# Product keys: the output product of the last group in two column ranges, and batch 14 weighed on VectorE

## The chip, the cores and the metric

One Trainium2 chip, one of its cores. The metric is the device time of one execution in microseconds (us), the median of several. The core has five engines with a queue each: TensorE (PE in the profile; PEld is its weight load), VectorE (DVE), ScalarE (ACT), GpSimd (POOL) and SyncE (SP).

## The reference, cut to what matters

The kernel is four layers of cross attention and feed-forward on x (16 batches of 128 tokens of 128 numbers). The change touches one stage, the feed-forward part of layer 2, which looks up experts by product keys:

```python
def _L2_ffn_ref(x, w_q, keys, expert_down, expert_up, norm_w):
    xn = _rmsnorm(x, norm_w)                                   # 2048 tokens x 128
    q = (xn @ w_q.T).reshape(b, t, H, 2, DK)                   # H=8 heads, two halves
    sim1 = jnp.einsum('bthd,hkd->bthk', q[..., 0, :], keys[:, :, 0, :])   # 32 keys
    sim2 = jnp.einsum('bthd,hkd->bthk', q[..., 1, :], keys[:, :, 1, :])   # 32 keys
    s1, i1 = jax.lax.top_k(sim1, K)
    s2, i2 = jax.lax.top_k(sim2, K)
    # the K*K sums s1+s2, of which the K best pairs (k1, k2) pick experts 32*k1 + k2
    wd = expert_down[fi]
    wu = expert_up[fi]
    hidden = jax.nn.gelu(jnp.einsum('btd,bthkd->bthk', xn, wd), approximate=False)
    hidden = hidden * jax.nn.relu(fs)
    return jnp.einsum('bthk,bthkd->btd', hidden, wu)
```

## The kernel before

The program is a chain of stages, each a block of its own: the engines' queues are joined at the end of one, and the next begins when all are through. The stage here is `product_keys` (l2f in the names). It computes the hidden value of all 1024 experts for each token, weighs each with what the chosen pairs give it, and multiplies the result by the 1024 x 128 output matrix.

Names: B = 16 batches, in four groups g of GB = 4 (batch b is number q = b % 4 of group b // 4). K = 32 keys a side, and P = S = D = 128. Per batch b:

- PE `score(b)` (line 2569) makes the similarities. DVE and POOL pick the eight best of each side and the threshold of the pairs (`tops`, `parts`, `threshold`, `compare`, and the tensor_tensor operations of POOL), and DVE turns the factors of both sides (`turn`, lines 2804 and 2810).
- ACT `spread(b)` (line 2663) copies the right factor into four diagonal blocks. It waits for the turn and for the `give` before (`given_made`), since `blocks` is one buffer.
- PE `give(b)` (line 2593) multiplies both factors: 32 matmuls in fp32, into `given_ps`, one buffer, so it also waits until batch b - 1 has been read out of it.
- The weighing multiplies `hid[g % 2][:, :, q, :]` by `given_ps`. Batches with q = 0 and 3 are weighed by DVE straight from PSUM (line 2781). Those with q = 1 and 2 (`ON_POOL`) go by way of ACT, which copies `given_ps` to SBUF (`store_given`, line 2669), and POOL multiplies (line 2714).
- `hide(g, c)` (line 2580) and ACT's Gelu make the hidden values of a whole group ahead of it.
- When the four batches of a group are weighed, PE `project_out(g)` (line 2605) multiplies by the output matrix: 32 keys k, and for each the four row groups j of 32 partitions, 128 matmuls with weights of 32 x 128 (`w["up"][rows, k, :]`) and 128 moving columns (four batches of 32 columns), summed over k in four banks of PSUM. ACT `store_out` (line 2677) copies the four banks, PE `finish(g)` (line 2616) transposes, DVE `add(g)` (line 2817, with the row statistics at lines 120 and 123) adds to x.

The order on each engine is written by hand, by rounds i = 0 to 19 (`ROUNDS`): in round i DVE does `parts`, `threshold` and `compare` of batch i, weighs batch i - 2, and turns batch i. PE gives batch i - 1. `project_out(3)` stands in round 17, `finish(3)` in round 18. `work_ps` has four banks, which `hid`, `out` and `finish` uses take in turn (`uses`, `place`, `wait_free`); the last use of a bank before `project_out(3)` is `finish(2)`, which `add(2)` on DVE frees. An fp32 matmul stands in the trace as two records of PE and two of PEld: 128 matmuls are x256.

Of the kernel before, what the change touches and what calls it, by code (L numbers as in the profile page):

```python
# [13 lines left out]
B, S, D = 16, 128, 128  # L14
# [14 lines left out]
NCH = B * S // CH  # L29
# [2423 lines left out]
def product_keys(nc, m, w, tag, meanwhile):  # L2453

    H, K, GB, TERMS = 8, 32, 4, 4
    KK, WORK = K // GB, 4
    ON_POOL = (1, 2)
    FAR = 1.0e30
    x, xnT, identity = m["x"], m["xnT"], m["identity"]
    with cleared_semaphores(nc) as new_semaphore, ExitStack() as ctx:  # L2460
# [63 lines left out]
        def bank(use):  # L2524
            return work_ps[place[use] % WORK]

        def wait_free(eng, use):
            n = place[use]
            if n >= WORK:
                eng.wait_ge(work_freed[n % WORK], n // WORK)  # L2530
# [13 lines left out]
        def exists(b):  # L2544
            return 0 <= b < B

        def on_pool(b):
            return b % GB in ON_POOL

        def count(b, pool):  # L2550
            return sum(on_pool(c) == pool for c in range(b))
# [9 lines left out]
        @block.tensor  # L2561
        def _(pe):
            mm = nc.tensor.matmul

            def score(b):
                norm.wait_stored(pe, b // GB)
                if b >= 2:
                    pe.wait_ge(parts_made, b - 1)
                mm(sim_ps[b % 2].rearrange("p h j k -> p (h j k)"), xnT[:, b, :], m["fold"][:, :],  # L2569
                   start=True, stop=True).then_inc(sim_made, 1)  # L2570

            def hide(g, c):
                use = ("hid", g, c)
                wait_free(pe, use)
                if g == 0 and c == 2:
                    norm.wait_stored(pe, NCH - 1)
                tokens = xnT[:, GB * g:GB * g + GB, :].rearrange("p q (u j s) -> p j (q u) s", u=4, j=4)
                for k in range(4):
                    for j in range(4):
                        ins = mm(bank(use)[K * j:K * j + K, k, :], w["down"][:, 4 * c + k, :], tokens[:, j],  # L2580
                                 start=True, stop=True)
                fill(ins, use)

            def give(b):
                pe.wait_ge(left_turned, b + 1)
                pe.wait_ge(blocks_made, 4 * b + 4)
                if b and on_pool(b - 1):
                    pe.wait_ge(given_stored, count(b, True))
                elif b:
                    pe.wait_ge(weighted, count(b, False))  # L2590
                for s in range(8):
                    for j in range(4):
                        ins = mm(given_ps[K * j:K * j + K, s, :, :], left_t[b % 2][:, 8 * j + s, :],  # L2593
                                 blocks[:, 8 * j + s, :, :], start=True, stop=True)
                ins.then_inc(given_made, 1)

            def project_out(g):
                for j in range(4):
                    wait_free(pe, ("out", g, j))
                pe.wait_ge(weighted, count(GB * g + GB, False))  # L2600
                pe.wait_ge(weighted_pool, count(GB * g + GB, True))
                for k in range(K):
                    for j in range(4):
                        rows = slice(K * j, K * j + K)
                        ins = mm(bank(("out", g, j))[:, 0, :], w["up"][rows, k, :], hid[g % 2][rows, k, :, :],
                                 start=(k == 0), stop=(k == K - 1))
                        if k == K - 1:
                            fill(ins, ("out", g, j))

            def finish(g):  # L2610
                use = ("finish", g, 0)
                for j in range(4):
                    wait_freed(pe, ("out", g, j))
                wait_free(pe, use)
                for q in range(GB):
                    ins = nc.tensor.transpose(bank(use)[:, q, :], out_t[:, q, :], identity[:, :])
                fill(ins, use)

            norm.pe(pe, 0)
            norm.pe(pe, 1)  # L2620
            score(0)
            norm.pe(pe, 2)
            norm.pe(pe, 3)
            score(1)
            for c in range(KK):
                hide(0, c)
            for i in ROUNDS:
                for g, c in chunks(i):
                    hide(g, c)
                if exists(i + 2):  # L2630
                    score(i + 2)
                if exists(i - 1):
                    give(i - 1)
                if out_group(i) is not None:
                    project_out(out_group(i))
                if i and out_group(i - 1) is not None:
                    finish(out_group(i - 1))
# [60 lines left out]
        @block.gpsimd  # L2698
        def _(pool):
            TT = nc.gpsimd.tensor_tensor  # L2700

            def wide(a):
                return a.unsqueeze(2).broadcast_to([P, H, 2, K])

            def each(a):
                return a.unsqueeze(3).broadcast_to([P, H, 2, K])

            def weigh(b):
                g, q = b // GB, b % GB
                if q == ON_POOL[0]:  # L2710
                    gelu_done(pool, b)
                pool.wait_ge(given_stored, count(b + 1, True))
                hidden = hid[g % 2][:, :, q, :].rearrange("p k (u s) -> p k u s", u=4)
                TT(hidden, hidden, given_sb.rearrange("p s u k -> p k u s"), ALU.mult).then_inc(weighted_pool, 1)

            norm.pool(pool)
            nc.gpsimd.memset(pairs[:, :, 28:36], 0.0).then_inc(zeroed, 1)
            nc.gpsimd.memset(blocks[:, :, :, :], 0.0).then_inc(zeroed, 1)
            for b in range(B):
                pool.wait_ge(top_made, b + 1)  # L2720
                if b:
                    pool.wait_ge(best_made, b)
                TT(pairs[:, :, 0:16].rearrange("p h (a c) -> p h a c", a=2),
                   top[:, :, 0, 0:2].unsqueeze(3).broadcast_to([P, H, 2, 8]),
                   top[:, :, 1, :].unsqueeze(2).broadcast_to([P, H, 2, 8]), ALU.add).then_inc(pairs_made, 1)
                TT(pairs[:, :, 16:28].rearrange("p h (a c) -> p h a c", a=6),
                   top[:, :, 0, 2:8].unsqueeze(3).broadcast_to([P, H, 6, 2]),
                   top[:, :, 1, 0:2].unsqueeze(2).broadcast_to([P, H, 6, 2]), ALU.add).then_inc(pairs_made, 1)
                if b:
                    pool.wait_ge(right_turned, b)  # L2730
                    pool.wait_ge(left_turned, b)
                TT(factors[:, 1, :, 0:2 * K].rearrange("p h (f k) -> p h f k", k=K),
                   wide(second_sim[b % 2][:, :, :]), each(top[:, :, 0, 0:2]), ALU.add).then_inc(sums_made, 1)
                pool.wait_ge(parts_made, b + 1)
                TT(factors[:, 0, :, 2 * K:4 * K].rearrange("p h (f k) -> p h f k", k=K),
                   wide(others[:, :, :]), each(top[:, :, 1, 0:2]), ALU.add).then_inc(sums_made, 1)
                for n, side in enumerate((1, 0)):
                    hot = factors[:, side, :, 2 * K * side:2 * K * side + K]
                    second = factors[:, side, :, 2 * K * side + K:2 * K * side + 2 * K]
                    TT(second, second, hot, ALU.subtract).then_inc(split_made, 1)  # L2740
                    value = factors[:, side, :, 2 * K * (1 - side):2 * K * (1 - side) + 2 * K]
                    pool.wait_ge(kept_made, 2 * b + n + 1)
                    TT(value, value, kept[:, side, :, :], ALU.mult).then_inc(cut_made, 1)  # L2743
                if exists(b - 2) and on_pool(b - 2):
                    weigh(b - 2)
            weigh(B - 2)
            row_stats.scale_known(pool)

        @block.vector
        def _(dve):  # L2750
# [72 lines left out]
            for i in ROUNDS:  # L2823
                if exists(i):
                    parts(i)
                    threshold(i)
                    compare(i)
                if exists(i - 2) and not on_pool(i - 2):
                    weigh(i - 2)
                if exists(i + 1):  # L2830
                    tops(i + 1)
                if exists(i):
                    turn(i)
                if i >= 2 and out_group(i - 2) is not None:
                    add(out_group(i - 2))


# [297 lines left out]
```

## Time and profile before

| | us |
|---|---|
| median of 3 runs | 1182.0 |
| lowest, highest | 1180.79, 1188.72 |
| the profiled execution | 1187.32 |
| its span (first to last instruction) | 1185.6 |
| the stage `product_keys` in it | about 840 to 1047 |

The rows further down are times of the profiled execution, counted from the start of its span. "x64" counts records, "mean ns" or "min/median/max" is the duration of one record. A released wait is printed behind a row in brackets with the instruction that ended it.

### The profile page before, as it was taken

What the parts mean: (1) busy time and instruction counts of PE and PEld (TensorE: products, weight loads), DVE (VectorE), ACT (ScalarE), POOL (GpSimd) and SP (SyncE); (2) the same over time, 40 slices, a digit from 0 to 9 for tenths busy, and PEclk for the clock granted to TensorE, in tenths of its full rate; (3) what the DMA queues carried; (4) which work ended last, traced back from release to release, by engine and by line L of the source; (5) the groups of instructions that cost most, each with busy time, mean ns of one, the idle gap of its engine ahead of it and who ended that gap; (6) DMA issues with size and microseconds to landing.
All of it is one profiled execution on the core that took longest, in us unless ns stands there. A gap on an engine that the chain in (4) does not pass through costs nothing. (4 is left out here: it accounts for less than half of the span.)

```text
span 1185.6 us, 26637 instructions
## 1 busy us (share of the span) xinstructions
PE 948.0 (80%) x10747; PEld 617.9 (52%) x10777; DVE 740.0 (62%) x2026; ACT 583.8 (49%) x956; POOL 414.4 (35%) x426
## 2 busy tenths in 40 slices
PE   3999799998999986998798781777556677479997
PEld 1577433443333433677676381445345555446776
DVE  3587747557455564654375233478899999636764
ACT  3365365535555344554563460377555555325442
POOL 4230300000000011676201656246578878623340
PEclk9799699998999998999898796899778987789997
DMA  6000000000000007000000132100000000000001
GB/s 268 1 3 2 19 1 0 1 1 0 1 1 1 0 1 288 10 2 3 2 3 2 36 110 56 72 1 1 1 2 2 2 2 3 2 1 2 2 2 37
DMA packets 15434, 27.95 MB, mean 24 GB/s; under 512 B 1104, under 2 KB 13264, under 8 KB 14544
## 3 DMA queue, kind: packets, MB, share of 16 engines
q1 hardware_dynamic: 14288, 24.14, 5.7%
q0 software_dynamic: 1024, 2.10, 0.6%
q8 instruction: 87, 1.43, 0.5%
q14 instruction: 35, 0.29, 0.1%
HBM read 20.33 MB, written 5.90 MB: 22 GB/s over the span
## 5 line engine op out<-in xcount | busy, mean ns | idle before, releaser
L1324 PE MATMUL l0f_ctl<-l1f_in,l0f_in 128*128 128x512 f32 x320 | 145.7, 599 | 0.5
L128 POOL TENSOR_SCALAR row_var_eps<-row_mean_var 128x12 f32<-128x12 f32 (+2 forms) x16 | 3.7, 230 | 358.5 <-DVE row_mean_var L123 357.7
L548 DVE TENSOR_REDUCE l_neg_max<-l_ring 128x4 f32<-128x512 f32 x128 | 82.1, 684 | 66.1 <-PE l_ring L410 65.6
L507 ACT ACTIVATE l_probs<-l_scores 128x1024 f32<-128x1024 f32 x64 | 65.6, 1025 | 82.2 <-PE l_scores L418 82.2
L2663 ACT COPY l2f_blocks_sb<-l2f_right_t_sb 32x1024 f32<-32x1024 f32 x64 | 66.8, 1044 | 68.2 <-DVE l2f_right_t_sb L2804 33.8
L1324 PEld LDWEIGHTS l0f_ctl<-l1f_in,l0f_in 128*128 128x128 f32 x320 | 61.7, 193 | 71.5 <-issue 70.2
L2593 PE MATMUL l2f_given_ps<-l2f_blocks_sb,l2f_left_t_sb 128*32 128x128 f32 x1024 | 47.8, 364 | 33.1 <-ACT l1f_in L2669 22.6
L698 POOL TENSOR_TENSOR l_squares<-l_exps 128x1024 f32<-128x1024 f32 x32 | 60.6, 1895 | 29.8 <-ACT l_exps L953 29.8
L2593 PEld LDWEIGHTS l2f_given_ps<-l2f_blocks_sb,l2f_left_t_sb 128*32 128x32 f32 x1024 | 42.8, 150 | 47.1 <-issue 46.9
L1045 DVE TENSOR_REDUCE l_neg_max<-l_scores 128x8 f32<-128x1024 f32 x32 | 39.2, 1225 | 43.4 <-PE l_scores L750 43.4
L368 POOL TENSOR_SCALAR_AFFINE_SELECT l_probs<-l_probs 128x1024 f32<-128x1024 f32 x32 | 35.0, 1094 | 64.1 <-ACT l_probs L507 64.1
L1597 DVE TENSOR_SCALAR l0f_halt<-l0f_halt 128x512 f32<-128x512 f32 x8 | 3.4, 427 | 78.8 <-ACT l0f_halt L1483 78.8
L1590 DVE SCALAR_TENSOR_TENSOR l1f_in<-l0f_index,l0f_in,l0f_hidden 128x512 f32<-128x512 bf16 x64 | 43.5, 747 | 12.3 <-ACT l0f_index L1464 11.1
L2743 POOL TENSOR_TENSOR l2f_factors_sb<-l2f_factors_sb,l1f_in 128x512 f32<-128x512 f32 x32 | 48.0, 1500 | 0.0
L953 ACT ACTIVATE l_exps<-l_scores 128x1024 f32<-128x1024 f32 x32 | 32.8, 1025 | 30.0 <-PE l_scores L756 29.8
L410 PE MATMUL l_ring<-l_k_heads,l_q_all 32*128 32x256 f32 x256 | 41.0, 441 | 7.9 <-issue 3.2
L1324 PE MATMUL l0f_work<-xnT,l0f_in 128*128 128x512 f32 (+2 forms) x88 | 45.0, 684 | 1.3 <-ACT xnT L204 0.7
L750 PE MATMUL l_scores<-l_k_heads,l_q_all 32*128 32x256 f32 x256 | 36.8, 402 | 10.0 <-DVE l_neg_max L1045 8.3
L2569 PE MATMUL l2f_sim_ps<-l1f_in,xnT 128*128 128x512 f32 x32 | 21.6, 764 | 28.8 <-DVE l1f_in L2772 28.8
L1446 ACT ACTIVATE l0f_hidden<-l0f_work,l0f_in 128x512 f32<-128x512 f32 (+1 forms) x40 | 27.3, 686 | 29.0 <-PE l0f_work L1324 29.0
L992 ACT ACTIVATE l_exps<-l_scores 128x1024 f32<-128x1024 f32 x32 | 31.0, 1021 | 20.7 <-PE l_scores L837 20.7
L756 PE MATMUL l_scores<-l_q_all,l_k_heads 32*128 32x128 f32 x512 | 37.7, 286 | 1.8 <-ACT l_exps L953 1.8
(458 smaller groups left out, 2610.2 us busy)
## 6 DMA issues: line engine op xcount, KB each, us to landing
l1f_in<-in_l1f SPq DMA_DIRECT2D x1, 4580.0 KB, 13.4
l0f_in<-in_l0f SPq DMA_DIRECT2D x1, 2302.5 KB, 8.9
l0f_in<-in_l2f SPq DMA_DIRECT2D x1, 2080.5 KB, 18.7
l1f_in<-in_l2u SPq DMA_DIRECT2D x1, 2048.0 KB, 8.6
sorted_rows<-first_in SPq DMA_DIRECT2D x1, 1856.0 KB, 11.2
l1f_sorted<-sorted_rows SPq DMA_DIRECT2D x7, 256.0 KB, 4.6
expert_rows<-l1f_sorted SPq DMA_DIRECT2D x7, 256.0 KB, 2.2
x_in<-in_x SPq DMA_DIRECT2D x1, 1024.0 KB, 5.0
```

The lines of the kernel that those rows point to most:

```text
L410: ins1 = mm(score_bank(b, half, g)[:, :, t, :], q_all[r, b, t, :], k_heads[r, b, t, :, :], start=not causal, stop=True, skip_group_check=True)
L507: nc.scalar.activation(probs[c % 2][:, 2 * pair:2 * pair + 2], scores2[:, :, :, :, :], ACT.Exp, scale=SCORE_SCALE).then_inc(exp_done, 1)
L548: ring.free(V.tensor_reduce(out, score_bank(b, half, g), AX.X, ALU.max, negate=True), ("score", b, half, g))
L698: nc.gpsimd.tensor_tensor(squares[c % 2][:, pair], e, e, ALU.mult).then_inc(squared, 1)
L750: ins1 = mm(scores1[:, g, :, t, :], q_all[r, b, t, :], k_heads[r, b, t, :, :], start=True, stop=True, skip_group_check=True)
L756: ins2 = mm(scores2[:, g, j, t, :], k_heads[r, c, t, j, :], q_all[r, c, t, :], start=True, stop=True, skip_group_check=True)
L1045: V.tensor_reduce(out, scores1[:, :, :, :, :].rearrange("p g j t s -> p (g j) t s"), AX.X, ALU.max, negate=True).then_inc(max_taken, 1)
L1324: return nc.tensor.matmul(out, lhs, rhs, start=start, stop=stop)
L1590: ins = STT(chosen[c % 2][:, k, p, :], index[k][:, c % 2, :], w["row_expert"][:, p:p + 1], hidden[c % 2][:, p, :], ALU.is_equal, ALU.mult)
L2593: ins = mm(given_ps[K * j:K * j + K, s, :, :], left_t[b % 2][:, 8 * j + s, :], blocks[:, 8 * j + s, :, :], start=True, stop=True)
L2663: A.copy(blocks[rows, :, u, :], right_t[rows, :, :]).then_inc(blocks_made, 1)
L2743: TT(value, value, kept[:, side, :, :], ALU.mult).then_inc(cut_made, 1)
```

## The change

Three things are changed. Batch 14 (q = 2 of the last group) is weighed by DVE, and the copy on ACT and the multiplication on POOL for it are gone. DVE's `add(2)` moves from round 15 to round 16, behind that weighing. `project_out(3)` becomes three calls: the columns of batches 12 to 14 for keys 0 to 11 (`EARLY_KEYS`) in round 16 ahead of `give(15)`; the same columns for keys 12 to 31 in round 17, behind `give(15)`; and the 32 columns of batch 15 for all 32 keys behind that. The four banks are waited for by the first call, and each call waits for the weighing of its own batches.

```diff
-    ON_POOL = (1, 2)
+    ON_POOL, EARLY_KEYS = (1, 2), 12
...
         def on_pool(b):
-            return b % GB in ON_POOL
+            return b % GB in ON_POOL and b != B - 2
...
-            def project_out(g):
-                for j in range(4):
-                    wait_free(pe, ("out", g, j))
-                pe.wait_ge(weighted, count(GB * g + GB, False))
-                pe.wait_ge(weighted_pool, count(GB * g + GB, True))
-                for k in range(K):
+            def project_out(g, batches=range(GB), keys=range(K)):
+                if batches[0] == 0 and keys[0] == 0:
+                    for j in range(4):
+                        wait_free(pe, ("out", g, j))
+                pe.wait_ge(weighted, count(GB * g + batches[-1] + 1, False))
+                pe.wait_ge(weighted_pool, count(GB * g + batches[-1] + 1, True))
+                some = slice(batches[0], batches[-1] + 1)
+                cols = slice(K * batches[0], K * batches[-1] + K)
+                for k in keys:
                     for j in range(4):
                         rows = slice(K * j, K * j + K)
-                        ins = mm(bank(("out", g, j))[:, 0, :], w["up"][rows, k, :], hid[g % 2][rows, k, :, :],
+                        ins = mm(bank(("out", g, j))[:, 0, cols], w["up"][rows, k, :], hid[g % 2][rows, k, some, :],
                                  start=(k == 0), stop=(k == K - 1))
-                        if k == K - 1:
+                        if k == K - 1 and batches[-1] == GB - 1:
                             fill(ins, ("out", g, j))
...
+                if i == B:
+                    project_out(NCH - 1, range(GB - 1), range(EARLY_KEYS))
                 if exists(i - 1):
                     give(i - 1)
-                if out_group(i) is not None:
+                if out_group(i) == NCH - 1:
+                    project_out(NCH - 1, range(GB - 1), range(EARLY_KEYS, K))
+                    project_out(NCH - 1, range(GB - 1, GB))
+                elif out_group(i) is not None:
                     project_out(out_group(i))
...
-            weigh(B - 2)
             row_stats.scale_known(pool)
...
-                if i >= 2 and out_group(i - 2) is not None:
+                if i == B:
+                    add(out_group(i - 3))
+                elif i >= 2 and out_group(i - 2) is not None and i != B - 1:
                     add(out_group(i - 2))
```

PE's queue at the end of the stage, before, from the `give` of batch 13 on (rows are line, operation, output<-inputs, shape, count; `l2f_given_ps` is written by `give`, `l2f_work_ps` by `project_out` and `finish`):

```order
L2593 MATMUL l2f_given_ps<-l2f_blocks_sb,l2f_left_t_sb 32x128 x32
L2616 MATMUL l2f_work_ps<-first_in,l1f_in 128x128 x4
L2593 MATMUL l2f_given_ps<-l2f_blocks_sb,l2f_left_t_sb 32x128 x64
L2605 MATMUL l2f_work_ps<-l2f_hid_sb,l1f_in 128x128 x128
L2616 MATMUL l2f_work_ps<-first_in,l1f_in 128x128 x4
L2460 UNCONDITIONAL_BRANCH
```

The same place now; the line numbers have moved by three:

```order
L2593 MATMUL l2f_given_ps<-l2f_blocks_sb,l2f_left_t_sb 32x128 x32
L2619 MATMUL l2f_work_ps<-first_in,l1f_in 128x128 x4
L2593 MATMUL l2f_given_ps<-l2f_blocks_sb,l2f_left_t_sb 32x128 x32
L2608 MATMUL l2f_work_ps<-l2f_hid_sb,l1f_in 128x96 x48
L2593 MATMUL l2f_given_ps<-l2f_blocks_sb,l2f_left_t_sb 32x128 x32
L2608 MATMUL l2f_work_ps<-l2f_hid_sb,l1f_in 128x96 x80
L2608 MATMUL l2f_work_ps<-l2f_hid_sb,l1f_in 128x32 x128
L2619 MATMUL l2f_work_ps<-first_in,l1f_in 128x128 x4
L2460 UNCONDITIONAL_BRANCH
```

Forty-eight matmuls of 96 columns stand ahead of the last `give` (batch 15), and behind it the 128 matmuls of the output product have become 80 of 96 columns and 128 of 32 columns.

DVE's queue at the end of the stage, before, from the turn of batch 15 on:

```order
L2804 STREAM_TRANSPOSE l2f_right_t_sb<-l2f_factors_sb 128x32x32
L2810 STREAM_TRANSPOSE l2f_left_t_sb<-l2f_factors_sb 128x32x32
L2817 TENSOR_TENSOR x_in<-x_in,l2f_work_ps 128x512
L120 BN_STATS row_stats<-x_in 128x6 x4
L123 BN_AGGR row_mean_var<-row_stats 128x2 x4
L2781 TENSOR_TENSOR l2f_hid_sb<-l2f_hid_sb,l2f_given_ps 128x32x32
```

and now, where lines 2788, 2811, 2817 and 2824 are the former 2781, 2804, 2810 and 2817:

```order
L2811 STREAM_TRANSPOSE l2f_right_t_sb<-l2f_factors_sb 128x32x32
L2817 STREAM_TRANSPOSE l2f_left_t_sb<-l2f_factors_sb 128x32x32
L2788 TENSOR_TENSOR l2f_hid_sb<-l2f_hid_sb,l2f_given_ps 128x32x32
L2824 TENSOR_TENSOR x_in<-x_in,l2f_work_ps 128x512
L120 BN_STATS row_stats<-x_in 128x6 x4
L123 BN_AGGR row_mean_var<-row_stats 128x2 x4
L2788 TENSOR_TENSOR l2f_hid_sb<-l2f_hid_sb,l2f_given_ps 128x32x32
```

The weighing of batch 14 has come in between the turn of batch 15 and `add(2)`; the weighing of batch 15 is last in both.

## Rows read from the trace of the kernel before

**Rows 1.** The page: busy us of each engine, share of the span, instructions.

```profile
PE 948.0 (80%) x10747; PEld 617.9 (52%) x10777; DVE 740.0 (62%) x2026; ACT 583.8 (49%) x956; POOL 414.4 (35%) x426
```

**Rows 2.** Stretches of the stage: us, busy per engine (records), granted clock, DMA.

```profile
840.00:1047.10 207.10, 135.06 (x3136) 110.38 (x3136) 185.03 (x553) 105.28 (x144) 151.19 (x144) 0.83 0.01 2
1019.70:1029.70 10.00, 3.52 (x64) 3.21 (x64) 7.12 (x13) 5.18 (x5) 7.16 (x6) 0.67 0.01 2
```

**Rows 3.** The timeline, PE, end of the stage: start us, us, what [idle before].

```profile
1019.82 3.52 PE L2593 MATMUL l2f_given_ps<-l2f_blocks_sb,l2f_left_t_sb 128*32 128x128 f32 x64 [6.36 <-ACT l1f_in L2669]
1029.76 3.64 PE L2593 MATMUL l2f_given_ps<-l2f_blocks_sb,l2f_left_t_sb 128*32 128x128 f32 x64 [6.41 <-ACT l1f_in L2669]
1034.92 7.43 PE L2605 MATMUL l2f_work_ps<-l2f_hid_sb,l1f_in 32*128 32x128 f32 x256 [1.53 <-DVE l2f_hid_sb L2781]
1043.53 0.60 PE L2616 MATMUL l2f_work_ps<-first_in,l1f_in 128*128 128x128 f32 x4 [1.18 <-ACT l1f_in L2677]
```

**Rows 4.** The timeline, DVE, the same stretch and the next stage's start.

```profile
1024.18 2.08 DVE L2810 STREAM_TRANSPOSE l2f_left_t_sb<-l2f_factors_sb 128x1024 f32<-128x1024 f32 x1
1026.11 0.70 DVE L2817 TENSOR_TENSOR x_in<-x_in,l2f_work_ps 128x512 f32<-128x512 f32 x1
...
1033.45 1.22 DVE L2781 TENSOR_TENSOR l2f_hid_sb<-l2f_hid_sb,l2f_given_ps 128x1024 f32<-128x1024 f32 x1 [5.33 <-PE l2f_given_ps L2593]
1044.16 0.69 DVE L2817 TENSOR_TENSOR x_in<-x_in,l2f_work_ps 128x512 f32<-128x512 f32 x1 [9.49 <-PE l2f_work_ps L2616]
...
1047.14 3.73 DVE L179 TENSOR_SCALAR l_probs<-x_in,row_mean_var,row_rstd 128x128 f32<-128x128 f32 x13 [0.98 <-PEq L43]
```

**Rows 5.** The timeline, ACT, the same stretch.

```profile
1024.33 4.25 ACT L2663 COPY l2f_blocks_sb<-l2f_right_t_sb 32x1024 f32<-32x1024 f32 x4 [4.65 <-DVE l2f_right_t_sb L2804]
1028.60 1.01 ACT L2669 COPY l1f_in<-l2f_given_ps 128x1024 f32<-128x1024 f32 x1
1042.39 0.78 ACT L2677 COPY l1f_in<-l2f_work_ps 128x128 f32<-128x128 f32 x4 [12.78 <-PE l2f_work_ps L2605]
```

**Rows 6.** The timeline, POOL, the same stretch: batch 13, batch 14, statistics.

```profile
1023.96 2.89 POOL L2714 TENSOR_TENSOR l2f_hid_sb<-l2f_hid_sb,l1f_in 128x1024 f32<-128x1024 f32 x1
1029.69 2.87 POOL L2714 TENSOR_TENSOR l2f_hid_sb<-l2f_hid_sb,l1f_in 128x1024 f32<-128x1024 f32 x1 [2.84 <-ACT l1f_in L2669]
...
1032.93 2.29 POOL L131 TENSOR_TENSOR row_rstd<-row_var_eps,first_in 128x12 f32<-128x12 f32 x1
```

**Rows 7.** Short stretches (columns as in rows 2): the granted clock.

```profile
1023.00:1023.40 0.40, 0.34 (x11) 0.01 (x1) 0.40 (x1) 0.00 (x0) 0.40 (x1) 0.89 0.00 0
1026.50:1027.00 0.50, 0.00 (x0) 0.00 (x0) 0.47 (x2) 0.50 (x1) 0.35 (x1) 0.50 0.00 0
1033.00:1033.40 0.40, 0.40 (x8) 0.00 (x0) 0.00 (x0) 0.00 (x0) 0.40 (x1) 0.59 0.00 0
1034.90:1042.30 7.40, 7.38 (x256) 7.26 (x256) 0.00 (x0) 0.00 (x0) 0.32 (x1) 1.00 0.02 4
```

**Rows 8.** The timeline, PE: a `give` in a busy stretch.

```profile
968.80 1.96 PE L2593 MATMUL l2f_given_ps<-l2f_blocks_sb,l2f_left_t_sb 128*32 128x128 f32 x64
```

**Rows 9.** The timeline, PE: weights of 128 x 128, moving 128 and 32.

```profile
1169.96 1.50 PE L2046 MATMUL l3f_turn_ps<-l3f_in,xnT 128*128 128x128 f32 x12
825.11 3.76 PE L2330 MATMUL l_counts<-l0f_in 128*128 128x32 f32 x32
```

**Rows 10.** One line's forms (durations min/median/max): two weight loads and a short matmul.

```profile
L2605 PEld LDWEIGHTS l2f_work_ps<-l2f_hid_sb,l1f_in x1024: 181/187/333, 912.5 to 1042.0; 32*128 32x128 f32 x171
L2330 PEld LDWEIGHTS l_counts<-l0f_in x32: 191/192/272, 825.0 to 828.5; 128*128 128x128 f32 x32
L1324 PE MATMUL l0f_ctl<-l0f_in,l0f_route x32: 356/356/378, 140.3 to 142.7; 32*128 32x8 f32 x32
```

**Rows 11.** Short stretches of line 1324 alone: us, PE, PEld, granted clock, DMA.

```profile
141.40:141.60 0.20, 0.20 (x11) 0.20 (x10) 0.50 0.00 0
141.60:141.80 0.20, 0.20 (x10) 0.20 (x12) 0.50 0.00 0
```

## The prediction

> **What bounds the kernel now.** The page comes first: PE is the busiest engine, at 80% of the span [rows 1]. That is an average over many stages, so the stretches of the stage come next: from 840 to 1047 us DVE is busy for 185 of 207 us and PE for 135 [rows 2]. In the rounds DVE leads, but the change touches only their end, and there the timeline of each engine has to be read side by side. The reader should see one chain with nothing beside it. PE gives batch 15 from 1029.76 to 1033.40 [rows 3]; DVE weighs it from 1033.45 to 1034.67 after 5.33 us of idleness [rows 4]; PE starts the output product at 1034.92, 0.25 us later, and ends at 1042.35 [rows 3]; ACT copies at 1042.39 [rows 5]; PE transposes at 1043.53 [rows 3]; DVE adds at 1044.16, and the next stage's first work on DVE is at 1047.14 [rows 4]. The queues are joined there, so whatever moves the end of the output product moves everything after it by as much. In the chain stand two stretches in which PE sits idle, 6.41 us ahead of the last `give` and 1.53 us ahead of the product, and one slow piece: the `give` takes 3.64 us, against 1.96 us for the same 64 records in a busy stretch [rows 3, 8]. The granted clock is 0.50 (1.2 GHz) after the idle time and 1.00 (2.4 GHz) in the whole of the output product [rows 7].
>
> **The copy and POOL's product for batch 14.** `give` of batch 15 waits for `given_ps` to be free. The copy on ACT that frees it stands behind `spread`, from 1028.60 to 1029.61, and PE starts 0.15 us after it [rows 3, 5]. With DVE reading `given_ps` instead, the `give` would be ready when `spread` ends, 1028.58 [rows 5], so at about 1028.7: 1.05 us earlier. POOL loses 2.87 us that ended at 1032.56, while the batch after it was not weighed until 1034.67 [rows 4, 6]: worth nothing. DVE gains one weighing of 1.22 us, which fits into its 5.33 us of idleness [rows 4]: it costs nothing itself.
>
> **The weighing of batch 14 and `add(2)` on DVE.** The factors are turned by 1026.1, when `add(2)` starts now [rows 4], and the `give` of batch 14 is through at 1023.34 [rows 3]. So DVE weighs from 1026.1 to 1027.3 and adds to 1028.0 (0.70 us). Behind it the statistics end near 1029.3, and POOL needs 2.5 us from them (its last row takes 2.29 us [rows 6]), done by 1032: hidden by 14 us of other work.
>
> **The early piece.** It waits for the weighing of batch 14 and for its four banks, the last of which `add(2)` frees at 1028.0. With the 0.25 us seen between DVE and PE [rows 3, 4] it starts at 1028.2, half a us before `give` of batch 15 would be ready. It stands ahead of the `give` in PE's queue, so all of it delays the `give`. It has 48 matmuls, 96 records. What is one worth? The 256 records of the output product take 7.43 us; their weight loads stand 28 ns apart ((7.26 - 0.187) / 255) [rows 3, 7, 10]. At half clock that is 53 ns: the short matmuls of line 1324 last 356 ns each, and 10 or 11 of them are to be seen in a stretch of 0.20 us at clock 0.50, so a new one starts every (200 + 356) / 10.5 = 53 ns [rows 10, 11].
>
> The clock fell to 0.50 by 1026.50 [rows 7], so the early piece starts at half speed. After the start at 1019.82 the stretch up to 1023.40 shows a mean of 0.89, so 78% of it is at full clock: the first 3.3 us of that `give` ran at half clock. Of the next one, from 1029.76, the mean of 0.59 makes it the first 3.6 us [rows 3, 7]. I take 3.4 us of half clock here too, up to 1031.6. Until then 3.4 / 0.053 = 64 records go through, the other 32 take 0.9 us, and the `give` can follow at 1032.5. It then runs at full clock: 1.96 us instead of 3.64 [rows 3, 8]. It ends at about 1034.4, **1.0 us later** than before. The bounds: at full clock from the first record the early piece takes 2.7 us and the `give` ends at 1032.8 (0.6 us earlier); at half clock throughout it takes 5.1 us and the `give` ends at 1035.2 (1.8 us later).
>
> **The rest of the output product.** Before, 8.95 us lay between the end of `give` and the end of the product: 1.52 us for the weighing and 7.43 us of PE. Now the 80 matmuls of 96 columns follow the `give` at once, and the weighing of batch 15 (1.5 us with its hand-overs) hides behind them. But the last piece is again 128 matmuls, 256 records, each with a weight load of its own. Whether it takes a quarter of the time because it moves a quarter of the columns, or the same time, is the question that decides this change. The trace of before has no matmul with 32 rows of weights and 32 columns. The nearest rows all say that the weight load sets the pace. A full 128 x 128 load with 128 moving columns takes 1.50 us for 12 records, and with 32 moving columns 3.76 us for 32 [rows 9]: less the last record's length (some 0.28 us) 111 and 112 ns each. The columns make no difference. A load of 32 rows lasts 187 ns against 191 for 128 rows [rows 10], so fewer rows don't shorten it either; the four row groups load side by side, and 112 / 4 = 28 ns is what the product shows. And line 1324 with only 8 moving columns keeps 53 ns at half clock, twice 27 [rows 10, 11]. So I take 28 ns for both widths: 160 records 4.5 us, 256 records 7.2 us, and 0.1 us for the last record's end, 11.8 us in place of 8.95: **2.85 us more**. The splitting adds 256 records to 256, takes 96 of them out ahead of the `give`, and saves only 1.5 us of waiting. The bounds of this term: by columns alone (21 and 7 ns) it is 5.3 us, 3.65 less than before; with each load and its columns one after the other it is 16.1 us, 7.15 more.
>
> The Trainium skill (TensorE: Matmul & The Clock Gate, section "Wait — 56ns, not 53.3ns?") says that matmuls never start closer than about 25 ns however few columns they have. By it alone the last piece would be 6.4 us, and the sum 0.8 us smaller. No row here has so short a matmul at full clock in all four row groups, so this trace neither confirms nor refutes the figure.
>
> **The sum.** The product ends 1.0 + 2.85 = 3.85 us later, near 1046.2 instead of 1042.35. The copies, transposes, addition and join behind it are the same. Against the profiled execution (1187.32, span 1185.6) this gives 1191.2; that execution was 5.3 us above the median of 1182.0, and the same difference on the median gives **1185.8 us**. With the bounds of the clock alone the difference is 2.2 to 4.7 us.
>
> **The rivals.** *Columns set the price* (the change ends faster): if a record of the output product costs its columns, 96 cost 21 ns and 32 cost 7 ns (40 ns for 96 at half clock). The early piece then ends near 1031.8 and the `give` near 1033.8, 0.4 us later than before, and the rest takes 5.3 us: 0.4 - 3.65 = 3.25 us faster, 1178.8 us. For it speaks that with 128 columns the load and the columns may well take equally long, so that the 28 ns of the product alone can't tell which of them it is; against it, rows 9 and 11. The Trainium skill gives this rival in the same page, section Back-to-back issue gap: the isolated gap at full clock is N / 2.4 + 2.5 ns, which falls with the columns. The rows 9 speak against using it where every matmul loads weights.
>
> *Loads come into the open* (clearly slower): with few columns to stream, the next load of the same row group may no longer lie beside them. Each record would cost its load and its columns in turn: 47 ns for 96 and 34 ns for 32, 16.1 us for the rest, and some 2 us more in the early piece: about 10 us slower in all, 1192 us. It decides if the product's records after `give` stand over 30 ns apart. The equal spacing of 128 and 32 columns at a full load [rows 9] speaks against it.
>
> *The net is nothing*: if the clock is granted soon after the early piece begins and the records go somewhat closer than 28 ns, the loss is 0 to 2 us and can't be seen: 1183 us. That the change does nothing at all is excluded, since PE's queue is different.
>
> **How the numbers follow.** My forecast has a chance of 0.72, columns 0.12, the net of nothing 0.09, open loads 0.04; 0.03 is left for a change of the clock in later stages. The three runs of before lie 7.9 us apart, so the median of after can miss by 2 or 3 us without a cause. The range of 1179 to 1191 takes in the forecast with the bounds of the clock, the net of nothing and most of the columns' case. A difference within 1% (12 us) can't be told from none by so few runs, and none of the cases but an upset beyond them reaches it: faster 0.02, same 0.95, slower 0.03.
>
> **What would show it.** In the profile after: the early piece at 1028 us or so, 96 records in 4 to 5 us at a clock that begins at 0.50; the `give` behind it near 2 us instead of 3.64; DVE's last weighing inside the 96-column stretch, with no idle PE between; the two stretches behind the `give` at 4.5 and 7.2 us; the end of the product some 12 us after the `give`. If the 256 records of 32 columns take 2 us, or over 8, the step on weight loads is wrong. If the early piece takes under 3 us, the one on the clock is.

## The result, and the profile after

The changed kernel took 1194.4 us in the median (four runs, 1191.2 to 1202.7) against 1182.7 for the kernel before: a ratio of 1.0086 with a 95% interval of 1.0049 to 1.0123 (the two medians by themselves stand 0.99% apart). Measured once more among the experiments it was 1.0046 (1.0015 to 1.0077). Neither interval holds 1, so the changed kernel is slower, by some 0.5 to 0.9%, 5.4 to 10 us. The forecast was 1185.8, a loss of 3.85 us, with a range from 1179 to 1191: the sign was right, the loss about one and a half to two and a half times as large as said. One execution whose trace is read below, that of the wide last piece, was 1.6% slower than the fastest of its kernel, so only what lies within the stage is read from it.

The end of the stage in the trace of the changed kernel, PE first (start us, us, what, idle before it and its releaser). These rows answer to [rows 3]. The row of 416 records merges the 96-column and the 32-column matmuls behind the `give`.

```profile
1015.93 3.53 PE L2593 MATMUL l2f_given_ps<-l2f_blocks_sb,l2f_left_t_sb 128*32 128x128 f32 x64 [6.35 <-ACT l1f_in L2677]
1024.37 5.33 PE L2608 MATMUL l2f_work_ps<-l2f_hid_sb,l1f_in 32*128 32x96 f32 x96 [4.91 <-DVE x_in L2824]
1029.63 1.96 PE L2593 MATMUL l2f_given_ps<-l2f_blocks_sb,l2f_left_t_sb 128*32 128x128 f32 x64
1031.52 15.01 PE L2608 MATMUL l2f_work_ps<-l2f_hid_sb,l1f_in 32*128 32x96 f32 x416
1047.61 1.08 PE L2619 MATMUL l2f_work_ps<-first_in,l1f_in 128*128 128x128 f32 x4 [1.09 <-ACT l1f_in L2685]
```

DVE in the same stretch, which answers to [rows 4]:

```profile
1022.24 1.17 DVE L2788 TENSOR_TENSOR l2f_hid_sb<-l2f_hid_sb,l2f_given_ps 128x1024 f32<-128x1024 f32 x1
1023.34 0.67 DVE L2824 TENSOR_TENSOR x_in<-x_in,l2f_work_ps 128x512 f32<-128x512 f32 x1
...
1031.66 1.22 DVE L2788 TENSOR_TENSOR l2f_hid_sb<-l2f_hid_sb,l2f_given_ps 128x1024 f32<-128x1024 f32 x1 [6.33 <-PE l2f_given_ps L2593]
1048.73 0.69 DVE L2824 TENSOR_TENSOR x_in<-x_in,l2f_work_ps 128x512 f32<-128x512 f32 x1 [15.86 <-PE l2f_work_ps L2619]
...
1051.72 6.78 DVE L179 TENSOR_SCALAR l_probs<-x_in,row_mean_var,row_rstd 128x128 f32<-128x128 f32 x13 [0.98 <-PEq L43]
```

The two profiled executions reach this place at different times, so the ruler for everything below is a distance within a trace: from the start of the `give` of batch 14 to the end of the output product. Before, it is 1019.82 to 1042.35, 22.5 us [rows 3]; after, it is 1015.93 to 1046.53, 30.6 us: 8.1 us more. Another 0.4 us is lost behind it, from there to the next stage's first work on DVE (4.8 us before, 5.2 us after), since the four transposes take 1.08 us instead of 0.60. That makes 8.5 us. The span grew by only 3.9 us, because the stage had begun 4.1 us earlier in that execution (DVE's first work in it at 836.31, before at 840.42) and the later stages took 0.7 us less. The code of those stages is the same in both kernels, so this is the spread between executions. The stage by itself took 206.7 us before (DVE's first work at 840.42, that of the next stage at 1047.14) and 215.4 us in both profiles of the changed kernel: 8.7 us more.

Where the 8.1 us went is seen in short stretches of the same trace (us; PE, PEld, DVE, ACT, POOL busy with records; granted clock; DMA): the early piece, the `give`, the 96 columns, and then the 32 columns in three stretches.

```profile
1024.30:1029.40 5.10, 5.03 (x95) 5.06 (x96) 0.99 (x8) 0.37 (x1) 2.48 (x2) 0.50 0.01 3
1029.60:1031.50 1.90, 1.90 (x68) 1.69 (x64) 0.00 (x0) 0.00 (x0) 0.00 (x0) 1.00 0.00 0
1031.50:1036.00 4.50, 4.50 (x164) 4.48 (x164) 1.22 (x1) 0.00 (x0) 0.00 (x0) 1.00 0.01 4
1036.00:1039.50 3.50, 3.50 (x139) 3.50 (x132) 0.00 (x0) 0.00 (x0) 0.00 (x0) 1.00 0.02 5
1039.50:1040.50 1.00, 1.00 (x32) 1.00 (x31) 0.00 (x0) 0.00 (x0) 0.00 (x0) 0.60 0.06 16
1040.50:1046.50 6.00, 6.00 (x116) 5.89 (x112) 0.00 (x0) 0.00 (x0) 0.00 (x0) 0.50 0.00 0
```

The granted clock, third from the right, is the thing to read. PE is busy for the whole of the last three stretches, with nothing to wait for, and the clock still falls from 1.00 to 0.50 near 1039.7, 3.7 us after the 32-column matmuls began. Until then 132 loads go through in 3.5 us, 27 ns each; afterwards 112 in 6 us, 53 to 54 ns each. The instructions of the product's line show it in the length of one load, first between 1037 and 1039, then between 1041 and 1046 (durations in ns min/median/max, first and last start):

```profile
L2608 PEld LDWEIGHTS l2f_work_ps<-l2f_hid_sb,l1f_in x78: 187/187/187, 1036.9 to 1039.0; 32*128 32x128 f32 x78
```

```profile
L2608 PEld LDWEIGHTS l2f_work_ps<-l2f_hid_sb,l1f_in x100: 328/328/328, 1040.7 to 1045.8; 32*128 32x128 f32 x100
```

### The profile page after: what moved, and what is told of

It reads as the page before. It is cut to its first block and busy times, and to the rows that moved or that the text cites. A ratio compares the mean times of both kernels' runs of the same rounds, so it can differ in the third digit from the quotient of the medians.

```text
span 1189.5 us, 27179 instructions
## 1 busy us (share of the span) xinstructions
PE 955.2 (80%) x11033; PEld 626.1 (53%) x11033; DVE 743.9 (63%) x2027; ACT 582.2 (49%) x955; POOL 410.8 (35%) x425
## 5 line engine op out<-in xcount | busy, mean ns | idle before, releaser
L2608 PE MATMUL l2f_work_ps<-l2f_hid_sb,l1f_in 32*128 32x128 f32 (+2 forms) x1280 | 43.4, 297 | 4.9 <-DVE x_in L2824 4.9
L2608 PEld LDWEIGHTS l2f_work_ps<-l2f_hid_sb,l1f_in 32*128 32x128 f32 x1280 | 42.5, 214 | 6.4 <-issue 6.4
L992 ACT ACTIVATE l_exps<-l_scores 128x1024 f32<-128x1024 f32 x32 | 31.0, 1021 | 20.7 <-PE l_scores L837 20.6
## 6 DMA issues: line engine op xcount, KB each, us to landing
l1f_in<-in_l1f SPq DMA_DIRECT2D x1, 4580.0 KB, 13.6
```

Source lines behind the costliest of these rows:

```text
L2608: ins = mm(bank(("out", g, j))[:, 0, cols], w["up"][rows, k, :], hid[g % 2][rows, k, some, :], start=(k == 0), stop=(k == K - 1))
```

## The experiments

The theory after the first look: the weight loads set the pace at either clock, as forecast, and the loss beyond the forecast is the clock, which falls under the 32-column matmuls although PE never pauses. The rivals: the early piece costs the time, DVE's extra weighing does, the columns themselves cost, or the clock falls by the length of the busy stretch and not by the kind of matmul. All distances are from the traces, one execution each; the ratios are those of the timed runs to the kernel before, measured anew beside them, with 95% intervals. All of them lie within 1% of the kernel before, so what is read from a ratio is whether its interval leaves out 1.

| run | distance, us | ratio (interval) |
|---|---|---|
| before | 22.5 | |
| changed | 30.6 | 1.0086 (1.0049 to 1.0123) |
| whole product | 23.0 | 0.9989 (0.9964 to 1.0013) |
| wide last piece (128) | 29.3 | 1.0060 (1.0024 to 1.0096) |
| no early piece | 30.6 | 1.0060 (1.0031 to 1.0090) |
| whole product, filler | 19.8 | 0.9954 (0.9927 to 0.9981) |
| last piece of 64 columns | 27.4 | 1.0020 (0.9982 to 1.0058) |
| before, with filler | 20.9 | 0.9945 (0.9908 to 0.9981) |
| filler and split | 26.4 | 1.0053 (1.0020 to 1.0087) |
| changed, again | 30.6 | 1.0046 (1.0015 to 1.0077) |

**The whole product, with DVE's weighing of batch 14.**

```diff
-                if i == B:
-                    project_out(NCH - 1, range(GB - 1), range(EARLY_KEYS))
...
-                if out_group(i) == NCH - 1:
-                    project_out(NCH - 1, range(GB - 1), range(EARLY_KEYS, K))
-                    project_out(NCH - 1, range(GB - 1, GB))
-                elif out_group(i) is not None:
+                if out_group(i) is not None:
```

> One part alone: batch 14 weighed by DVE and add(2) behind it, but the output product of the last group whole, 128 matmuls of 128 columns behind the weighing of batch 15. The measure is the distance in the trace from the start of the give of batch 14 to the end of the output product: 22.5 us in the kernel before (1019.82 to 1042.35), 30.6 us in the changed kernel (1015.93 to 1046.53). Theory 1 (all the loss is in the split of the product: 256 more records, and 32-column matmuls under which the granted clock falls): the last give starts 1.0 us earlier, at half clock, and the distance is 21.5 us; the whole kernel within 2 us of before. Rival (DVE's extra weighing or the moved add hurts): 22.5 us or more.

The distance was 23.0 us (1017.74 to 1040.76), the ratio 0.9989. PE's timeline:

```profile
1017.74 3.64 PE L2593 MATMUL l2f_given_ps<-l2f_blocks_sb,l2f_left_t_sb 128*32 128x128 f32 x64 [6.34 <-ACT l1f_in L2672]
1026.58 3.64 PE L2593 MATMUL l2f_given_ps<-l2f_blocks_sb,l2f_left_t_sb 128*32 128x128 f32 x64 [5.19 <-ACT l2f_blocks_sb L2666]
1031.74 9.02 PE L2608 MATMUL l2f_work_ps<-l2f_hid_sb,l1f_in 32*128 32x128 f32 x256 [1.53 <-DVE l2f_hid_sb L2783]
```

The last `give` now starts 8.8 us after the one before instead of 9.9, and its releaser is `spread` (the blocks) and not the copy: the 1.1 us are there. But the product took 9.02 us instead of 7.43, because the clock came later in this execution:

```profile
1026.50:1035.00 8.50, 6.89 (x124) 6.50 (x128) 1.82 (x7) 0.00 (x0) 2.49 (x2) 0.50 0.01 2
1035.00:1036.00 1.00, 1.00 (x40) 1.00 (x39) 0.00 (x0) 0.00 (x0) 0.00 (x0) 0.93 0.00 0
```

It was granted 8.5 us after the `give` began, against 3.6 us in the kernel before [rows 3, 7]. So the number expected, 21.5 us, was missed by 1.5 us, and the 1.6 us by which the product was longer account for it. By the distance alone the rival's mark (22.5 us or more) was reached; the rows speak against the rival, since the `give` came 1.1 us earlier and what was lost lies in PE's own records at 0.50. The ratio of 0.9989 agrees: DVE's weighing and the moved `add(2)` cost nothing that these runs can show, and the loss lies in the split.

**The wide last piece.** The same 256 records and loads, with all 128 columns into a free part of the banks; the copy takes the last 32 from there.

```diff
-                cols = slice(K * batches[0], K * batches[-1] + K)
+                cols, slot = slice(K * batches[0], K * batches[-1] + K), 0
+                if len(batches) == 1:
+                    some, cols, slot = slice(0, GB), slice(0, GB * K), 1
...
-                        ins = mm(bank(("out", g, j))[:, 0, cols], w["up"][rows, k, :], hid[g % 2][rows, k, some, :],
+                        ins = mm(bank(("out", g, j))[:, slot, cols], w["up"][rows, k, :], hid[g % 2][rows, k, some, :],
...
```

> The changed kernel, but the last piece streams all 128 columns into a free part of the same banks, and the copy takes only the 32 columns of batch 15 from there: the same 256 records and weight loads in the last piece, four times the columns. Four small copies more on ACT. Theory 1 (the weight loads set the pace at full clock, and the clock falls because 32 columns leave the array too idle): the clock stays 1.00 to the end, the last 256 records take 7.2 us in place of some 10.5, distance 27.3 us, the kernel about 3 us faster than the changed one. Rival 2 (the clock falls after so long a stretch of back-to-back loads whatever the columns): it falls near the same place, distance 30 us or more. Rival 3 (columns cost time): the last piece takes longer than 10.5 us.

The distance was 29.3 us (1018.49 to 1047.79).

```profile
1026.92 5.45 PE L2610 MATMUL l2f_work_ps<-l2f_hid_sb,l1f_in 32*128 32x96 f32 x96 [4.78 <-DVE x_in L2830]
1032.30 3.64 PE L2593 MATMUL l2f_given_ps<-l2f_blocks_sb,l2f_left_t_sb 128*32 128x128 f32 x64
1035.87 11.92 PE L2610 MATMUL l2f_work_ps<-l2f_hid_sb,l1f_in 32*128 32x96 f32 x416
```

and the last piece in the stretches:

```profile
1040.40:1047.80 7.40, 7.39 (x264) 7.20 (x260) 0.00 (x0) 0.00 (x0) 0.00 (x0) 1.00 0.02 4
```

The 416 records took 11.9 us instead of 15.0, very nearly the 11.8 us of the forecast, and the clock stayed at 1.00 to the end. Four times the columns, and 3.1 us less: this rules out that columns cost time here. It also speaks against the clock falling by the length of the stretch: from 1036.0 it stayed at 1.00 for 11.8 us, to the end of the product, while in the changed kernel it fell 10.2 us after it had risen. The distance missed the 27.3 us expected because the early piece this time didn't bring the clock: the `give` ran at half clock, 3.64 us instead of 1.96. The timed runs don't show the 3 us that were expected against the changed kernel: 1.0060 (1.0024 to 1.0096) here, 1.0086 and 1.0046 there.

**No early piece.**

```diff
-                if i == B:
-                    project_out(NCH - 1, range(GB - 1), range(EARLY_KEYS))
...
-                    project_out(NCH - 1, range(GB - 1), range(EARLY_KEYS, K))
+                    project_out(NCH - 1, range(GB - 1))
```

> The changed kernel without the early piece: all 128 matmuls of 96 columns behind the last give, then the 128 of 32 columns. Theory 1: the last give starts 8.9 us after the start of the one before and takes 3.6 us at half clock; 256 records of 96 columns at full clock 7.2 us; 256 of 32 columns about 10.5 us since the clock falls some 3.8 us after they begin; distance 30.3 us, much as the changed kernel: the early piece gains nothing and costs nothing. Rival (the early piece itself is what costs): distance 27 us or less.

The distance was 30.6 us (1019.27 to 1049.86), the same as with the early piece. The stretches, the first nearly all of 96 columns, the others of 32:

```profile
1033.00:1040.00 7.00, 7.00 (x261) 7.00 (x256) 0.01 (x1) 0.00 (x0) 0.00 (x0) 1.00 0.02 5
1040.00:1043.00 3.00, 3.00 (x116) 3.00 (x112) 0.00 (x0) 0.00 (x0) 0.00 (x0) 1.00 0.00 0
1043.00:1044.00 1.00, 1.00 (x28) 1.00 (x24) 0.00 (x0) 0.00 (x0) 0.00 (x0) 0.53 0.08 16
1044.00:1049.90 5.90, 5.86 (x112) 5.73 (x108) 0.00 (x0) 0.00 (x0) 0.00 (x0) 0.50 0.00 0
```

The early piece neither gains nor costs anything that can be seen beside the clock, which by itself moves the distance by 1.7 us between executions; the rival that the early piece is the trouble falls. The clock falls again in the 32 columns, here near 1043.1, 3.7 us after they began at 1039.4, and they take 10.5 us again.

**The filler: what the half clock of the last `give` is worth.** To the whole product with DVE's weighing come six matmuls nobody reads:

```diff
+                if i == B:
+                    wait_free(pe, ("out", NCH - 1, 0))
+                    for _ in range(6):
+                        mm(bank(("out", NCH - 1, 0)).rearrange("p q s -> p (q s)"), xnT[:, 0, :], m["fold"][:, :],
+                           start=True, stop=True)
                 if exists(i - 1):
                     give(i - 1)
```

> The whole product as in the first run, and six fp32 matmuls of 128 x 512 whose result nobody reads, ahead of the last give, where PE is idle. Theory (the last give is slow only because the clock has fallen in the idle time): it takes 1.96 us in place of 3.6, distance 19.8 us, the kernel some 2.7 us faster than before. Rival (the filler runs past the point where the give is ready, or the clock falls all the same): distance 21.5 us or more.

```profile
1020.88 5.42 PE L2638 MATMUL l2f_work_ps<-l1f_in,xnT 128*128 128x512 f32 x12
1026.25 1.96 PE L2593 MATMUL l2f_given_ps<-l2f_blocks_sb,l2f_left_t_sb 128*32 128x128 f32 x64
1029.73 7.43 PE L2608 MATMUL l2f_work_ps<-l2f_hid_sb,l1f_in 32*128 32x128 f32 x256 [1.53 <-DVE l2f_hid_sb L2788]
```

The distance was 19.8 us (1017.39 to 1037.16), as expected to a tenth, and the ratio 0.9954: faster than both kernels, by 5.5 us (2 to 9) against the one before where 2.7 were expected. In the kernel before the same filler was put in alone.

> The kernel before with nothing but the six unread matmuls ahead of the last give. Theory (filler and DVE's weighing are two separate gains): the last give still starts 9.9 us after the one before, since the copy on ACT is back in its way, but takes 1.96 us in place of 3.64; distance from give 14 to the end of the product 20.9 us, against 19.8 with DVE's weighing and 22.5 without either. Rival (the clock falls again in the microsecond between the filler and the give): 22.5 us.

```profile
1016.60 5.42 PE L2635 MATMUL l2f_work_ps<-l1f_in,xnT 128*128 128x512 f32 x12
1023.16 1.95 PE L2593 MATMUL l2f_given_ps<-l2f_blocks_sb,l2f_left_t_sb 128*32 128x128 f32 x64 [1.14 <-ACT l1f_in L2674]
```

20.9 us (1013.19 to 1034.08), as expected: the two gains of 1.1 us (the copy out of the way) and 1.7 us (the `give` at full clock) are separate. The clock held through the 1.14 us between the filler and the `give`, so the rival falls. The timed runs put this version at 0.9945, some 6 us less where the distance says 1.6. The rest is not accounted for. In the profiled execution it lies ahead of anything that was changed: the stage began at 833.58, against 840.42 in that of the kernel before. The interval (0.9908 to 0.9981) doesn't tell the two filler versions apart.

What the filler has over the early piece is when it starts. It waits for no result and follows the `give` of batch 14 at once, when the clock has just risen (it starts at 1020.88; the mean from 1020 to 1021 is 0.63, from then on 1.00). The early piece has to wait for DVE, starts 4.9 us after that `give`, and finds the clock back at 0.50 since about 1022.6. No run tells whether real work at the filler's place would do as much.

**The last piece of 64 columns.** As the wide last piece, with the columns of batches 14 and 15 (here the lines differ from those of the wide last piece):

```diff
-                    some, cols, slot = slice(0, GB), slice(0, GB * K), 1
+                    some, cols, slot = slice(2, GB), slice(2 * K, GB * K), 1
```

> The run with the wide last piece, with 64 moving columns there in place of 128 (of the batches 14 and 15, of which the second is kept). Theory 1 (the clock falls because too few columns stream between the loads): a value between the two seen is tried. If it is gradual the clock holds or falls later; if it holds, the last 256 records take 7.2 us. If it falls as with 32 columns, about 10.5 us. Rival (only the number of records or the time since the clock rose counts): it falls as with 32 columns, which the run with 128 columns already speaks against.

```profile
1037.00:1038.00 1.00, 1.00 (x36) 0.91 (x35) 0.00 (x0) 0.00 (x0) 0.00 (x0) 0.88 0.00 0
1039.30:1043.80 4.50, 4.50 (x165) 4.45 (x160) 1.22 (x1) 0.00 (x0) 0.00 (x0) 1.00 0.02 4
1043.80:1051.20 7.40, 7.39 (x268) 7.25 (x260) 0.00 (x0) 0.00 (x0) 0.00 (x0) 1.00 0.02 4
```

The clock held, the last piece took 7.4 us, the distance was 27.4 us (1023.80 to 1051.19), 3.2 us less than with 32 columns. The number of records and loads is the same in both, so these don't decide. The clock had risen near 1037.2 and was still at 1.00 when the product ended at 1051.19, 14 us later, so a fixed time since it rose doesn't decide either. The timed runs, 1.0020 (0.9982 to 1.0058) against 1.0046 for the changed kernel measured beside it, point the same way, but the intervals overlap.

**Filler and split together.** The changed kernel with the filler where the early piece was, and the 96 columns whole.

```diff
                 if i == B:
-                    project_out(NCH - 1, range(GB - 1), range(EARLY_KEYS))
+                    wait_free(pe, ("out", NCH - 1, 0))
+                    for _ in range(6):
...
-                    project_out(NCH - 1, range(GB - 1), range(EARLY_KEYS, K))
+                    project_out(NCH - 1, range(GB - 1))
```

> The changed kernel with the filler in place of the early piece, and all 128 matmuls of 96 columns behind the last give, then the 128 of 32. Theory 1: last give at full clock, 1.96 us; 7.2 us for the 96 columns; the clock falls 3.5 to 4 us into the 32 columns and they take about 10.5 us all the same; distance 28.5 us. Rival (the clock falls only because it was granted late or after an early piece at half clock): it holds, and the distance is 25 us.

```profile
1033.90:1039.00 5.10, 5.10 (x196) 5.10 (x188) 0.00 (x0) 0.00 (x0) 0.00 (x0) 1.00 0.02 6
1039.00:1040.00 1.00, 1.00 (x44) 1.00 (x40) 0.00 (x0) 0.00 (x0) 0.00 (x0) 0.91 0.00 0
1040.00:1042.50 2.50, 2.46 (x48) 2.33 (x44) 0.00 (x0) 0.00 (x0) 0.00 (x0) 0.50 0.03 7
```

The clock fell here too, after a long stretch at 1.00, but later than expected, 5.9 us into the 32 columns: they took 8.5 us, and the distance was 26.4 us where 28.5 were expected. So how the clock was won before doesn't protect it, and how much of the 32-column stretch is lost varies between executions. Even without any fall the split would end behind the whole product with the same filler: 14.3 us for 512 records against 9.0 us with the wait.

**The changed kernel once more.**

> The changed kernel once more, for a narrower interval and a second profile of it. Theory 1: the clock falls 3.5 to 4 us into the 32-column matmuls again, which take about 10.5 us; distance 30.6 us, or 1.7 us more where the clock isn't granted before the last give; slower than before by 8 to 10 us. Rival (the fall was a chance of that one execution): distance 27.3 us, slower by 4 to 5 us.

30.6 us again (1014.71 to 1045.35), as expected. The ratio of 1.0046 is 5.4 us (1.8 to 9.1), less than the 8 to 10 us expected of the timed runs and nearer the rival's 4 to 5; the trace decides against the rival. The 32 columns of this second profile:

```profile
1034.80:1038.00 3.20, 3.20 (x126) 3.20 (x123) 0.00 (x0) 0.00 (x0) 0.00 (x0) 1.00 0.03 5
1038.00:1039.00 1.00, 1.00 (x36) 1.00 (x32) 0.00 (x0) 0.00 (x0) 0.00 (x0) 0.69 0.00 0
1039.00:1045.40 6.40, 6.34 (x120) 6.21 (x118) 0.00 (x0) 0.01 (x1) 0.00 (x0) 0.50 0.01 3
```

The fall is no accident of one execution: all four traces with 32-column matmuls in the last piece have it, and neither of the two with 64 or 128 columns in their place does. One regularity is left: in three of the four (the changed kernel twice, no early piece) the clock fell 10.2 us after it had risen. With the filler and the split it fell after 20.5 us, and with 64 columns it hadn't after 14.

## Why the prediction was wrong

*The copy and DVE's weighing* were right. The whole product's trace shows the `give` 1.1 us earlier (1.05 forecast) and released by `spread`. The weighing of batch 14, `add(2)` and the statistics lie in DVE's idle time, and PE starts the early piece 8.4 us after the `give` of batch 14, as worked out (1028.2 less 1019.8).

*The early piece* was mis-sized. It took 5.3 us and not 4.3, because half clock lasted 5.1 us and not 3.4. With the `give` at 1.96 us, as forecast, that `give` ended 15.7 us after the start of the one before, against 13.6 in the kernel before: 2.1 us later, where 1.0 was said and 1.8 was given as the bound. I took 3.4 us from two rows of `give` alone. At the same place half clock then lasted 4.7 us after PE had begun again with no early piece, 5.0 and 5.1 in the two profiles of the changed kernel, 8.5 with the whole product (with a pause of 1.5 us in it) and 9.1 with the wide last piece (with none), so two rows were too few for a bound.

*The rest of the output product* is the step that failed. Of its 11.8 us the first piece was right: 4.5 us for 160 records of 96 columns. The weight loads do set the pace: some 27 ns at 32 columns as at 64, 96 and 128, so the rivals "columns set the price" and "loads come into the open" are both refuted, "the net is nothing" falls with the 8.1 us of both traces, and the main argument, that the split doubles the loads and so can't gain, holds. But I priced all 256 records of the last piece at full clock: "I take 28 ns for both widths". The clock fell 3.7 us into it, and the piece took 10.5 us instead of 7.2. The wide last piece and the one of 64 columns, with the same records and loads, took 7.4 us at 1.00. In the last piece nothing was changed but the number of moving columns and the part of the bank that they are written to, so I take the columns as the cause; that the place in the bank matters is not tested, but the 32-column matmuls of line 2330 further down, which write to another tile, lost the clock too. The total was 14.9 us against 8.95: 6.0 us more, where 2.85 were forecast. My own sign would have misled: I wrote that 256 records taking over 8 us would prove the step on weight loads wrong. They took 10.5 us, and that step was right; it was the price at half clock that I had left out.

The Trainium skill (TensorE: Matmul & The Clock Gate, section "Wait — 56ns, not 53.3ns?") has matmuls start no closer than about 25 ns however few columns they have. The trace at full clock comes near it, 27 ns at 32 columns. At half clock it is 53 ns, so here the spacing isn't a fixed number of ns; a quarter of the 111 to 112 ns of a full load [rows 9] gives the same 28 ns. Whether a floor of 25 ns lies just under it, no run here tells.

*The sum.* 2.1 + 6.0 = 8.1 us in place of 3.85, and 0.4 us of transposes at half clock behind it. The two timed ratios are 0.46% and 0.86%, 5.4 and 10 us; the 8.5 us of the trace lie between them and inside both intervals.

*What I overlooked* stood in the profile of before. I read line 2330 for the spacing of its 32-column matmuls [rows 9] and didn't ask what the clock did under them. Two stretches of the kernel before:

```profile
827.00:828.00 1.00, 1.00 (x11) 1.00 (x10) 0.96 (x8) 0.58 (x2) 0.00 (x0) 1.00 0.00 0
828.00:829.00 1.00, 0.87 (x7) 0.74 (x6) 0.94 (x4) 0.00 (x0) 0.66 (x1) 0.77 0.00 0
```

The mean of 0.77 in the second puts the fall near 828.5: 3.4 us after those matmuls had begun and 0.3 us before they ended, though PE had been busy without a pause since 825. And the 128x14 matmuls of line 1825, with 128 x 128 transposes between them and PE busy nearly all the time from 641.3, ran at half clock from end to end; this is the last of their stretches:

```profile
648.30:651.90 3.60, 3.52 (x18) 3.41 (x16) 0.04 (x1) 0.59 (x1) 0.00 (x0) 0.50 0.00 0
```

Either row should have made a falling clock a rival with a price of its own; it came to 3.3 us here. My other near row, the 8-column matmuls [rows 11], even stood at 0.50, and I only divided it by two.

*What stays open*: why half clock lasts 3.6 us in one execution and 9.1 in another after much the same work, why the clock fell 3.7 us into the 32 columns in three traces and 5.9 in the fourth, and why the timed runs of the kernel before with the filler are faster than its distance says.

## What to carry to other kernels

Splitting a matmul's moving columns to start part of it early doubles the weight loads, and where loads already set the pace nothing is saved, however narrow the late piece is; count loads, not columns, ahead of such a split. When short matmuls are the nearest rows for a price, read the granted clock under them as well as their spacing: a busy PE is no sign that it keeps its clock. Where PE idles ahead of a piece on the path, a few wide matmuls whose result nobody reads, started before the clock falls, can be worth more than real work that can only start after it: here 1.7 us of 22.5.

## What the runs showed of the hardware

- The granted clock falls from 1.00 to 0.50 (2.4 to 1.2 GHz) while PE is busy without a gap: under fp32 matmuls of 32 moving columns with a 32 x 128 weight load each, 3.6 to 3.7 us after they began in three traces and 5.9 us in a fourth. With 64 or 128 columns and the same loads it stayed at 1.00 for the 7.4 us.
- More columns, written to another part of the bank, made the same 256 records faster: 7.4 us with 64 or 128 columns; 10.5, 10.5, 10.6 and 8.5 us with 32.
- The weight load paces at both clocks: 27 to 28 ns from one 32 x 128 load to the next in four row groups at 1.00, with 32, 64, 96 or 128 moving columns, and 52 to 54 ns at 0.50, with 32, 96 or 128.
- Behind the early piece of 96 columns, fed without a gap, the clock was back after 5.1 us in one trace and was not after 5.4 us in another; the `give` behind it then took 1.96 or 3.64 us.
- Under six matmuls of 128 x 512 that began within 0.3 us of the clock's rise it stayed at 1.00 for their 5.4 us, and in one trace for the 1.14 us of idle PE behind them; with PE idle in their place it had fallen by 1026.50 in the kernel before [rows 7]. The `give` of 64 records took 1.95 us at 1.00, against 3.64 at 0.50.
